# First expert stage of a four-layer transformer kernel: weighing experts four at a time on VectorE, with sums on GpSimd

## The reference

```python
logits = jnp.einsum('bsd,ed->bse', x, router_w) + router_b
probs = jax.nn.softmax(logits, axis=-1)
weights = jnp.max(probs, axis=-1)
top1 = jnp.argmax(probs, axis=-1)
y_all = jnp.einsum('bsd,eod->bseo', x, expert_w) + expert_b
y = jnp.take_along_axis(y_all, top1[:, :, None, None], axis=2)[:, :, 0, :]
out = y * weights[:, :, None]
```

## Time and profile before

| | us |
|---|---|
| median of 3 runs | 1589.41 (1586.63 to 1589.45) |
| the profiled execution's own time | 1589.34 |
| its span in the profile | 1587.6 |
| TensorE busy (matmuls) | 1382.5 (87%) |
| VectorE busy | 839.1 (53%) |
| ScalarE busy | 728.7 (46%) |
| GpSimd busy | 147.1 (9%) |

### The profile page before, as it was taken

One profiled execution on the slowest core, in us unless ns is written; L12 is line 12 of the kernel. 1 busy time (PEld: TensorE's weight loads), 2 busy tenths in 40 slices (PEclk: granted clock), 3 DMA queues, 4 the chain that ended last, 5 costly groups with the idle time before them and its releaser, 6 DMA issues. The chain is left out here.

```text
span 1587.6 us, 27487 instructions
## 1 busy us (share of the span) xinstructions
PE 1382.5 (87%) x9061; PEld 1082.9 (68%) x9061; DVE 839.1 (53%) x2258; ACT 728.7 (46%) x1657; POOL 147.1 (9%) x256
## 2 busy tenths in 40 slices
PE   6765799999996799789999997984699996999995
PEld 5642477777775387579999986973477773666764
DVE  4549676677662554635555543447677762122224
ACT  4331677777762402245555552442355542333333
POOL 1010000000001000000000002005244421000000
PEclk9869899999996999879999997995699996999998
DMA  8000000000000000000000004002000000000000
GB/s 330 1 1 0 1 1 1 2 1 1 1 1 1 1 1 0 1 1 2 1 1 1 1 2 105 16 1 106 0 1 1 0 1 1 1 1 1 0 1 27
DMA packets 6429, 24.55 MB, mean 15 GB/s; under 512 B 797, under 2 KB 1311, under 8 KB 5418
## 3 DMA queue, kind: packets, MB, share of 16 engines
q1 hardware_dynamic: 6314, 23.03, 4.2%
HBM read 21.98 MB, written 1.05 MB: 15 GB/s over the span
## 5 line engine op out<-in xcount | busy, mean ns | idle before, releaser
L1306 DVE SCALAR_TENSOR_TENSOR XN<-bank,gate,XN 128x128 f32<-128x128 f32 x256 | 89.8, 351 | 224.7 <-PE bank L1270 222.2
L1286 ACT ACTIVATE e_hidden<-bank,small 128x512 f32<-128x512 f32 x152 | 104.4, 687 | 214.5 <-PE bank L1258 214.4
L766 PE MATMUL bank<-a_va,a_pT 128*128 128x65 f32 x1024 | 130.3, 270 | 0.7 <-ACT a_pT L933 0.6
L1011 DVE TENSOR_REDUCE a_mx<-bank 128x4 f32<-128x512 f32 x128 | 87.9, 686 | 80.0 <-PE bank L806 79.7
L1270 PEld LDWEIGHTS bank<-attention_weights,e_hidden 128*128 128x128 f32 x1024 | 119.2, 192 | 14.8 <-issue 14.8
L766 PEld LDWEIGHTS bank<-a_va,a_pT 128*128 128x128 f32 x1024 | 125.2, 193 | 2.5 <-ACT a_pT L933 1.1
L1258 PE MATMUL bank<-XNT,attention_weights 128*128 128x512 f32 x256 | 121.2, 606 | 1.2 <-PEq L541 1.2
L1270 PE MATMUL bank<-attention_weights,e_hidden 128*128 128x128 f32 x1024 | 119.3, 275 | 0.0
L831 PE MATMUL bank<-attention_weights,a_cv 128*128 128x256 f32 x256 | 84.4, 411 | 15.0 <-issue 15.0
L933 ACT ACTIVATE a_pT<-bank 128x512 f32<-128x512 f32 x128 | 76.1, 595 | 41.9 <-PE bank L840 39.2
L1019 DVE TENSOR_TENSOR a_shifted<-bank,a_mx 128x512 f32<-128x512 f32 x128 | 88.3, 690 | 3.4
(11 more groups left out here) (351 smaller groups left out, 2709.9 us busy)
## 6 DMA issues: line engine op xcount, KB each, us to landing
attention_weights<-in_a SPq DMA_DIRECT2D x2, 2048.0 KB, 11.8
mod_ring<-in_mod_weights SPq DMA_DIRECT2D x4, 576.0 KB
ctx_both<-in_ctx SPq DMA_DIRECT2D x1, 2048.0 KB, 9.5
attention_weights<-in_up SPq DMA_DIRECT2D x1, 2048.0 KB, 7.7
attention_weights<-in_down SPq DMA_DIRECT2D x1, 2048.0 KB, 13.7
down<-in_down SPq DMA_DIRECT2D x1, 1536.0 KB, 18.3
down<-in_mod_weights SPq DMA_DIRECT2D x2, 576.0 KB
X<-in_x SPq DMA_DIRECT2D x4, 256.0 KB, 3.9
```

Of the source, the lines that this page charges most:

```text
L766: last = pe.matmul(value_bank[:, j * (W + 1):(j + 1) * (W + 1)], pT[:, i.slot(2), j * 128:(j + 1) * 128], va[:, p, g // 2 * 8 + 2 * j + g ...
L1011: dve.tensor_reduce(mx[:, i.slot(2), :], score_bank[i.slot(2)][:, :].rearrange("p (h s) -> p h s", h=4), AX.X, ALU.max).then_inc(maxed, 1)
L1286: act.activation(hidden[0:rows, p, f, :], up_bank_of(i, f)[0:rows, :], function, bias=up_bias(g, f)).then_inc(hidden_ready, 1)
L1306: dve.scalar_tensor_tensor(out=total, in0=down_bank[j][:, e * D:(e + 1) * D], scalar=gate_column(k, 4 * q + j, g * per_group + e), in1=tot ...
```

## The change

The weighing and the summing of the experts are split. VectorE multiplies a whole bank (four experts of one batch) with the four gate columns, each broadcast over 128 columns, into a new SBUF buffer `e0_products` (two slots for pairs, two batches, two halves, 512 columns): four operations per pair. GpSimd adds the two halves of a batch in place (512 columns), then folds the sum to 256 columns into `e0_pairs`. VectorE adds the two remaining 128-column parts to `XN`, in two dependent operations per batch. TensorE's matmuls of the next pair now wait for the products, not for the sums. VectorE's order is: products of pair n, then additions of pair n - 1. GpSimd's order is: copy for pair n + 1, then for each batch of pair n addition and fold. VectorE's and GpSimd's streams are written out in full; TensorE's stays a loop.

```diff
@@ GpSimd
-            def body(at):
-                i = at(0)
-                n, p = i.number, i.slot(2)
-                if i.older_than(2):
-                    await_count(pool, experts_done, 4 * n - 4)
-                pool.tensor_copy(xs[:, p, :, :].rearrange("p a d -> p (a d)"),
+            def stage(n):
+                if n >= 2:
+                    pool.wait_ge(experts_done, 4 * n - 4)
+                pool.tensor_copy(xs[:, n % 2, :, :].rearrange("p a d -> p (a d)"),
                                  col(k.XNT, n, 256)).then_inc(staged, 1)
-            sweep(pool, PAIRS, 2, 0, body)
+
+            stage(0)
+            for n in range(PAIRS):
+                if n + 1 < PAIRS:
+                    stage(n + 1)
+                for a in range(2):
+                    half, p = products[:, n % 2, a, :, :], n % 2
+                    pool.wait_ge(weighed, 4 * n + a + 3)
+                    pool.tensor_tensor(half[:, 0, :], half[:, 0, :], half[:, 1, :], ALU.add).then_inc(fours_added, 1)
+                    pool.wait_ge(fours_added, 2 * n + a + 1)
+                    if n >= 2:
+                        pool.wait_ge(summed, 4 * n - 6 + 2 * a)
+                    pool.tensor_tensor(pairs[:, p, a, :], half[:, 0, 0:256], half[:, 0, 256:512],
+                                       ALU.add).then_inc(pairs_added, 1)
@@ TensorE
-                            await_count(pe, summed, 16 * n - 16 + 8 * half + 7 + a)
+                            await_count(pe, weighed, 4 * n - 3 + 2 * half + a)
@@ VectorE
-            def body(at):
-                i = at(0)
-                n = i.number
-                for e in range(E):
+            def weigh(n):
+                for half in range(2):
                     for a in range(2):
-                        if e % 4 == 0:
-                            await_count(dve, experts_done, 4 * n + e // 2 + a + 1)
-                        if e:
-                            await_count(dve, summed, 16 * n + 2 * e + a - 1)
-                        total = col(k.XN, 2 * n + a)
-                        dve.scalar_tensor_tensor(
-                            out=total, in0=k.ps[2 * (e // 4) + a][:, (e % 4) * 128:(e % 4 + 1) * 128],
-                            scalar=gate_column(k, 2 * n + a, e), in1=total, op0=ALU.mult,
-                            op1=ALU.add).then_inc(summed, 1)
-            sweep(dve, PAIRS, 2, 0, body)
+                        dve.wait_ge(experts_done, 4 * n + 2 * half + a + 1)
+                        if n >= 2:
+                            dve.wait_ge(pairs_added, 2 * n - 3 + a)
+                        dve.tensor_tensor(products[:, n % 2, a, half, :].rearrange("p (e d) -> p e d", e=4),
+                                          k.ps[2 * half + a][:, :].rearrange("p (e d) -> p e d", e=4),
+                                          k.gate[:, 2 * n + a, 4 * half:4 * half + 4].unsqueeze(2).to_broadcast([128, 4, D]),
+                                          ALU.mult).then_inc(weighed, 1)
+
+            def add(n):
+                for a in range(2):
+                    total = col(k.XN, 2 * n + a)
+                    dve.wait_ge(pairs_added, 2 * n + a + 1)
+                    dve.tensor_tensor(total, total, pairs[:, n % 2, a, 0:128], ALU.add).then_inc(summed, 1)
+                    dve.wait_ge(summed, 4 * n + 2 * a + 1)
+                    dve.tensor_tensor(total, total, pairs[:, n % 2, a, 128:256], ALU.add).then_inc(summed, 1)
+
+            for n in range(PAIRS):
+                weigh(n)
+                if n:
+                    add(n - 1)
+            add(PAIRS - 1)
             for q in range(4):
                 x = k.X[:, q * 512:(q + 1) * 512]
-                dve.wait_ge(summed, 16 * PAIRS)
+                dve.wait_ge(summed, 4 * PAIRS)
```

More of the change, by code:

```diff
@@ L609, in add_experts_0 @@
         stats = ctx.enter_context(nc.sbuf_tensor("e0_stats", [128, B, 6], F32))
+        products = ctx.enter_context(nc.sbuf_tensor("e0_products", [128, 2, 2, 2, 512], F32))
+        pairs = ctx.enter_context(nc.sbuf_tensor("e0_pairs", [128, 2, 2, 256], F32))
         staged, experts_done, summed = sem("staged"), sem("experts_done"), sem("summed")
+        weighed, fours_added, pairs_added = sem("weighed"), sem("fours_added"), sem("pairs_added")
         updated, sums_taken = sem("updated"), sem("sums_taken")
```

## The result

| | before | after |
|---|---|---|
| median of 6 runs, us | 1589.22 (1586.63 to 1590.13) | 1595.78 (1593.87 to 1596.73) |
| the profiled execution's own time | 1589.34 | 1593.87 |
| its span | 1587.6 | 1592.1 |
| the stage in the profile: first product to first wide update | 39.98 | 47.72 |

The ratio after to before is 1.0042, with a 95% interval of 1.0029 to 1.0055: slower by 0.42%, 6.6 us. The prediction was 1596.4, slower; the measured median lies 0.6 us from it, inside the stated range.

A forecast was written before the change was run, and what follows sets the result against it. VectorE's chain bounds the stage before (39.98 us); after the change VectorE's small additions and GpSimd's operations alternate, stretching it to 47.1 us. 1589.34 + 7.1 = 1596.4 us, range 1584.5 to 1602.

The forecast's parts named there:

- The lock and its alternation: VectorE's two-SBUF-input additions and GpSimd's additions and folds exclude each other; each small addition ends 0.15 us after one; chance 0.52.
- Rival 1: In the stage: GpSimd bound, operations this short do not block each other; -2.6 us, 1586.7 us; chance 0.15.
- Rival 2: In the stage: VectorE's additions slip in between, GpSimd pays up to 0.7 us a pair; +3.2, 1592.5 us; chance 0.16.
- rival 3: In the stage: VectorE bound, GpSimd's addition 1.04 and fold 0.61 us, slight blocking; -7.8, 1581.6 us; chance 0.10.
- Rival 4: In the stage: each GpSimd operation loses a full 0.28 us in the handover; +12, 1601.5 us; chance 0.07.
- The schedule: Hand-worked order of both engines through the eight pairs: 6.45 us a pair in step, stage 47.1 against 39.98, +7.1 us.
- 8 x 1.16: Saving over eight pairs were VectorE alone to count, 3.84 us a pair against 5.0: 9.2 us.
- x4, 1.96 us: Profile row at 126.47, taken as TensorE's four matmuls of a pair in 1.95 us, covered by VectorE's additions, costing nothing.
- the 3.9 us of the prediction: TensorE's four matmuls of a pair at half the clock, said to be still covered in a period of 6.45 us.
- GpSimd's copies don't contend: VectorE's small additions contend with GpSimd's additions and folds only; if copies blocked too, 0.4 to 1 us more.
- A1: First of VectorE's four small additions of a pair; for the first pair forecast to end 5.45 us after the first product.

The follow-up runs named there:

- version with three engines: Against the kernel before: VectorE fuses experts 0 to 3, ScalarE weighs 4 to 7, GpSimd folds those, VectorE joins four batches at a time; 1583.19 us, ratio 0.9969.
- one product, one addition: The changed kernel with only VectorE's order altered: each product is followed by one small addition; 1590.81 us, ratio to before 1.0011.
- VectorE alone: The changed kernel with VectorE also adding the halves and folding, GpSimd keeping only its copies; 1592.1 us, ratio to before 1.0027.
- wide additions: The changed kernel with two small additions of 256 columns per pair instead of four of 128; 1589.0 us, ratio to before 1.0004.
- runs with copies: The changed kernel with GpSimd's additions and folds replaced by copies of the same widths, sums left incomplete; 1581.49 us in a single execution.
- run with the multiplications: The changed kernel with GpSimd's additions and folds replaced by multiplications by 1.0, sums left incomplete; 1593.4 us in a single execution.

## Why the prediction was right

**What bounds the stage and what the engines need.** VectorE's products: 0.69 alone, four back to back in 2.47 (the row at 138.49), a step of 0.59 against 0.63 taken. GpSimd's addition: 1.26 undisturbed (1.26 taken), the fold, which no row had, 0.72 to 0.73 (0.72 taken). The small additions met nobody at the end and took 0.28.

**The lock and its alternation.** Shown by the run with the sums in PSUM: with one input and the result of the additions there, the stage falls by 10.0 us at unchanged counts and order. Three others agree: with half as many handovers it falls by 8.0, with products between the additions by 5.9, with no GpSimd arithmetic by 3.3. In step, each small addition ended 0.15 us after a GpSimd operation, as worked out from two rows of the kernel before, for operations four times as wide. Rival 1 failed on this: it held that operations of 128 columns are too short to block. Rivals 2, 3 and 4 failed on GpSimd's side: its additions and folds stayed at 1.26 to 1.31 and 0.72, and it idled.

**The schedule.** Period in step 6.16 against 6.45 forecast. The difference has three parts. The product's step was shorter (2 x 0.04 up to the third product, 0.07 measured). In the handovers GpSimd's addition lost 0.05 only once a pair (1.31) and the folds nothing (0.1 together). And the next products start 0.08 before the last addition ends, where I had them 0.03 behind it (0.1). The stage was 47.72 against 47.1: the products of pair 3 started 15.7 us into the stage instead of 13.3, and the shorter periods and a quicker end took 1.8 of these 2.4 back. So the mechanism and the period were right, but that the total came within 0.6 us is in part luck: two errors stood against each other. Two slips of the sums changed nothing: 8 x 1.16 is 9.3, not 9.2, and rival 3's GpSimd pair is 3.76, not 3.74.

**A term that was wrong.** The start was slower because TensorE's matmuls cost more than I said. The first eight products stand 0.86 us apart and each waits 0.17 for its bank:

```profile
110.42 0.69 DVE L670 TENSOR_TENSOR e_products<-bank,gate 128x512 f32<-128x512 f32 x1 [2.02 <-PE bank L654]
111.28 0.69 DVE L670 TENSOR_TENSOR e_products<-bank,gate 128x512 f32<-128x512 f32 x1 [0.17 <-PE bank L654]
```

I had read "x4, 1.96 us" as four matmuls. The stage has 32 matmuls and the profile lists 64: each float32 matmul of this kind has two records. So a pair costs TensorE 4 x 0.86 = 3.43 us, not 1.95, and the two first pairs ran at that pace: the first addition stands 6.6 us into the stage (117.03) instead of 5.2. The products of pair 2 came 1.3 late (9.2 against 7.95). GpSimd was only 0.5 late, so the additions of pair 1 now met four of its operations in a row, from its addition at 121.94 on, and the products of pair 3 came 2.4 late. In a period of 6.16 TensorE stayed covered, so the conclusion held with the wrong figure behind it. At a lower clock the cover was thinner than the 3.9 us of the prediction: with a granted clock of 0.68 four matmuls took 5.37 us (from 133.14), and still no product waited. In the version with three engines TensorE is the next bound.

**A second one.** "GpSimd's copies don't contend" was wrong, as two runs show. Here it cost little: A1 of the first pair waited for one (0.46 instead of 0.28), and in step the copy falls beside the last addition and takes 0.06 longer (0.46 instead of 0.40). The Trainium skill, "SBUF — State Buffer", section "Who interferes with whom", had it right that any GpSimd instruction that reads SBUF excludes a VectorE instruction with two SBUF inputs; the runs agree (0.53 beside a copy of 0.40). The prediction added from that section that the lock is held for the whole instruction; the section says this in its lines on VectorE's two-port modes. Here it is true of copies and additions, not of the multiplication by a constant: 0.62 of 1.49 us.

**The total.** The runs' medians against before follow their stages:

| run | stage less before's 39.98 | median less before's |
|---|---|---|
| the change | +7.7 | +6.6 |
| one product, one addition | +1.9 | +2.2 |
| VectorE alone | +4.4 | +3.5 |
| wide additions | -0.3 | +0.4 |
| sums in PSUM | -2.2 | -2.5 |
| three engines | -5.1 | -4.6 |

So next to nothing of the 7.7 us was hidden. The remaining difference of 1.1 us in the change's row isn't explained by any run. A stage is read from one profile each, and the profiled execution of "VectorE alone" was the fastest of its eight (1587.37), that of "one product, one addition" the slowest of its ten (1593.1); what they are off by stands outside the stage (1430.9 and 1436.6 us behind it). The runs with copies and with multiplications, executed once each, are not in the table.

## What to carry to other kernels

Before handing part of VectorE's work to GpSimd, count the VectorE operations left beside it that read two SBUF operands: each can be held until GpSimd's current copy or addition is over, and a chain of short ones advances one per GpSimd instruction. If they must stay, keep one operand in PSUM (0.29 us instead of 0.85 here, at the same count), make them few and wide, or put operations with a PSUM operand between them. Look for it in a trace as short VectorE operations that all end a fixed 0.15 us after GpSimd's.

## What the runs showed of the hardware that I had not expected

- GpSimd's multiplication by a constant (512 columns, 1.49 us) holds VectorE's two-input additions only for its first 0.62 us, that of 256 columns (0.85 us) for its first 0.40, in both cases the length of a copy of the same width. That it reads all its input in this time and then computes would explain it, but no run shows that.
- Additions of 128 columns in place in PSUM with one SBUF input cost VectorE 0.29 to 0.30 us, hardly more than those in SBUF (0.28 to 0.29).
- In the run with the multiplications, TensorE's granted clock was 0.72 from 118 to 124 us and again from 129 to 135 (means over both of its levels, 2.4 and 1.2 GHz). TensorE had stood idle for 2.04 us before the first (until 117.92) and for 1.92 before the second (until 128.67). Products then stood up to 1.7 us apart:

```profile
110.00:118.00 8.00, 5.96 (x15) 2.39 (x13) 6.75 (x12) 7.97 (x60) 5.43 (x6) 1.00 0.00 1
...
118.00:124.00 6.00, 6.00 (x10) 2.40 (x11) 3.08 (x6) 5.75 (x25) 5.65 (x6) 0.72 0.00 0
```

So here VectorE waited after TensorE's idle time for slower matmuls too. Idle time alone does not tell when that comes: in the changed kernel an idle time of 2.49 us was followed by a granted clock of 0.68 (133.14 to 138.51), and another of the same length by 1.00 (145.47 to 149.14). Its clock fell to 0.92 over the stage, against 1.00 before, and VectorE never waited for a bank after the first eight products.
